# Preparing rows two chunks ahead, and 22 halves of shared-expert units beside the first group's maxima

## The reference

```python
xn = _layernorm(x)
q, k, v = (split_heads(xn @ W + b) for W, b in ((Wq, bq), (Wk, bk), (Wv, bv)))
scores = jnp.einsum('bhqd,bhkd->bhqk', q, k) / jnp.sqrt(dk)      # causal, then softmax
attn_out = merge_heads(softmax(scores) @ v) @ Wo + bo
...
logits = xn @ gate_w.T                                           # 4096 rows, 16 experts
topk_w, topk_idx = top_k(softmax(logits), 4); topk_w /= topk_w.sum(-1)
y = sum over the 4 experts e of topk_w * (silu(xn @ w_gate[e]) * (xn @ w_up[e])) @ w_down[e]
y = y + (silu(xn @ sw_gate) * (xn @ sw_up)) @ sw_down
return x + attn_out + y
```

## Time and profile before

| what | value |
|---|---|
| median of 3 runs | 1351.32 us (1346.31 to 1351.62) |
| the profiled execution | 1356.54 us, of which the span from the first to the last instruction 1354.9 us |
| busy share of the span | PE 74%, DVE 64%, ACT 48%, POOL 43% |
| chain that ended last, by engine | PE 53%, DVE 10%, another core or an unknown queue 10%, issue 9% |
| moved by DMA | 126.41 MB, mean 93 GB/s |
| mean granted clock of PE | 0.88 of full speed |

### The profile page before, as it was taken

How to read it: one execution, slowest core, us unless ns; L and a number is a source line. 1 busy time by engine, 2 the same in 40 slices (tenths; PEclk the granted TensorE clock), 3 DMA queues, 4 the chain that set the end, 5 groups by cost and what they waited for, 6 DMA issues and landing times.

```text
span 1354.9 us, 26394 instructions
## 1 busy us (share of the span) xinstructions
PE 1007.9 (74%) x8634; PEld 525.7 (39%) x8634; DVE 866.0 (64%) x1784; ACT 654.5 (48%) x1219; POOL 579.2 (43%) x531
## 2 busy tenths in 40 slices
PE   2788121010399999898998989998988989899885
PEld 1555010000144444444544444454444445444433
DVE  6888831000288887777777676676767676677553
ACT  3778100000154545565566666556666665566341
POOL 6333177776200000454366666435656553464100
PEclk9888555555599999899999999999989999899888
DMA  6899450010113131443545355354535353444702
GB/s 175 270 297 283 125 180 1 1 34 1 43 56 105 54 104 48 88 85 75 89 80 112 63 111 95 66 89 78 111 57 112 56 112 64 88 71 73 134 17 31
DMA packets 99484, 126.41 MB, mean 93 GB/s; under 512 B 24873, under 2 KB 83514, under 8 KB 98834
## 3 DMA queue, kind: packets, MB, share of 16 engines
q0 software_dynamic: 41632, 60.79, 25.0%
q1 hardware_dynamic: 57730, 63.99, 16.1%
HBM read 71.63 MB, written 57.80 MB: 96 GB/s over the span
## 4 chain that ended last, share of the span: by engine, by line
PE 53%; DVE 10%; another core or an unknown queue 10%; issue 9%; ACT 2%; SPq 1%; DMA 1%; POOL 0%; ACTq 0%; DVEq 0%
PE gup L1221 12%; PE pvp L1144 10%; PE outs L1248 9%; DVE part L1314 6%; PE smp L1100 6%; PE turn L1233 4%; PE stp L1125 4%; PE outs L1151 3%; PE turn L1191 3%; PE smp L1083 1%; ACT probs L1484 1%; DVE hf L1371 1%; DVE sg L1366 1%; DMA Qs<-nm 1%
## 5 line engine op out<-in xcount | busy, mean ns | idle before, releaser
L1484 ACT ACTIVATE probs<-stp 128x1024 f32<-128x1024 f32 (+1 forms) x320 | 300.4, 939 | 424.4 <-remote 205.2
L1314 DVE TENSOR_REDUCE part<-smp 128x2 f32<-128x256 f32 (+2 forms) x372 | 345.9, 951 | 140.0 <-remote 72.5
L942 POOL DMA_INDIRECT XG<-xrow_d,slots x144 | 146.8, 1019 | 247.0 <-DMA out<-Y 201.7
L1221 PE MATMUL gup<-gu_w,XC 128*128 (+1 forms) x1152 | 212.8, 321 | 32.7 <-issue 21.8
L1100 PE MATMUL smp<-Ks,Qs 48*128 48x128 f16 (+2 forms) x744 | 112.5, 341 | 103.7 <-DVE part L1314 52.4
L1248 PE MATMUL outs<-dn_w,h 88*128 (+1 forms) x1248 | 183.6, 280 | 0.1
L949 POOL DMA_INDIRECT out<-Y,slots x72 | 117.1, 1626 | 139.1 <-ACT Y L1517 107.8
L1144 PE MATMUL pvp<-probs,Vs 128*32 128x512 f32 (+3 forms) x1536 | 168.8, 512 | 0.8 <-DVE probs L1413 0.7
L949 POOL DMA_INDIRECT acc_d<-Y,slots x72 | 114.7, 1594 | 123.7 <-ACT Y L1517 104.6
L1221 PEld LDWEIGHTS gup<-gu_w,XC 128*128 128x128 f16 x1152 | 107.2, 99 | 96.1 <-issue 43.5
L931 POOL DMA_INDIRECT slot_d<-entry,slot_i x128 | 124.3, 971 | 41.6 <-issue 41.6
(11 more groups left out here) (170 smaller groups left out, 1109.6 us busy)
## 6 DMA issues: line engine op xcount, KB each, us to landing
rb<-rsum_d SPq DMA_DIRECT2D x60, 128.0 KB
Ks<-k_d SPq DMA_DIRECT2D x96, 64.0 KB
Qs<-q_d SPq DMA_DIRECT2D x96, 64.0 KB
v_d<-V SPq DMA_DIRECT2D x8, 544.0 KB, 4.6
Vs<-v_d SPq DMA_DIRECT2D x16, 272.0 KB, 3.0
acc_d<-YA SPq DMA_DIRECT2D x1, 4224.0 KB
X<-L_attn_x POOLq DMA_DIRECT2D x8, 512.0 KB, 5.0
xrow_d<-XR SPq DMA_DIRECT2D x8, 512.0 KB, 5.0
```

The costliest lines, as they stand in the source:

```text
L942: pool.indirect_dma_start(XG[:, q].rearrange("p a c t -> p (a c t)"), None, s.xrow_d, bass.IndirectOffsetOnAxis(ap=slots[:, r, 0:1], axis= ...
L1221: last = pe.matmul(gup[:, 0:2 * I], columns[:, a, h], weights_of(s.gu_w, e, b, h, slice(0, 2 * I)), start=n == 0, stop=n == 5)
L1314: last = dve.tensor_reduce(part[:, g % 2, k0 // CH, :, j, t], banks[:, :, col:col + w], AX.X, ALU.max)
L1484: act.activation(to, of, ACT.Exp, scale=float(DK) ** -0.5 / QS ** 2).then_inc(exp_done, 1)
```

## The change

In the preparation:

- The loop is written out (eight steps in Python), so `wait_apart` and its counters are gone.
- Rows are normalised two chunks ahead (`normalise` and `rows_low` for c+2), variances three ahead.
- The four Newton operations are POOL's, in its list ahead of the loads that belong to the step.
- The memset of Ks on POOL (128x6144) is six of 128x1024, at chunks 0, 1, 6 and 7. A spare square root loads ACT's table at the start.
- The shared expert's weights are converted in step 0, two experts each in steps 1 to 5 and three each in the last two (`SPLITS`); both conversions of an expert stand at the end of a step.

In attention and experts:

- The first PRE = 22 halves (12 first halves, units 0 to 11, and 10 second halves, units 0 to 9) are taken out of the slots and put one each behind the 18 pieces of group 0 and four steps more. The turn of the maxima comes in step 19.
- The planner divides the other 394 halves over the 320 slots. The last shared first half waits for slot 50 at the earliest (`READY`).
- SP loads XC and xs first, then serves the halves, sends the maxima, and only then issues the clear of acc_d and the copy to out.

```diff
-            per_slot = (sum(cost) + sum(fixed_work(g, n) for g, n in every)) / (len(every) - SPARE)
             first, second, i, used = {}, {}, 0, 0
+            for m in range(PRE):
+                (first, second)[halves[i][0]][-1, m] = halves[i][1]
+                i += 1
+            per_slot = (sum(cost[i:]) + sum(fixed_work(g, n) for g, n in every)) / (len(every) - SPARE)
             for k, x in enumerate(every):
                 used += fixed_work(*x)
                 for _ in range(2):
+                    if k < READY and i < len(halves) and halves[i] == (0, SU - 1):
+                        continue
...
-        LAG, SPARE = 2, 4
+
+        LAG, SPARE, PRE, READY = 2, 4, MP + 4, 50
...
+            for t in range(2):
+                shared_columns(t)
+                shared_rows(t)
+            for m in range(MP):
+                after_halves(-1, m)
+            send_max(0)
             sp.wait_ge(a_const, 2)
             sp.dma_start(s.acc_d.rearrange("(t p) d -> p t d", p=P),
                          YA[:, 0:1].broadcast_to([P, TT + 1, D])).then_inc(cleared, 16)
             sp.dma_start(s.out[ST * P:T, :], s.xf[ST * P:T, :]).then_inc(cleared, 16)
-            for t in range(2):
-                shared_columns(t)
-                shared_rows(t)
-            send_max(0)
+            for m in range(MP, PRE):
+                after_halves(-1, m)
...
-            for m in range(MP):
-                max_piece(0, m, (smp, stp)[m % 2], m - 1)
-            turn_max(0)
-            pe.wait_ge(red_done, MP)
             projected = 0
             youts = 0
+            for m in range(PRE):
+                if m < MP:
+                    max_piece(0, m, (smp, stp)[m % 2], m - 1)
+                if m == MP + 1:
+                    turn_max(0)
+                if (-1, m) in FIRST:
+                    gate_up(FIRST[-1, m])
+                else:
+                    z = SECOND[-1, m]
+                    turn_h(z)
+                    if z:
+                        down(z - 1, projected)
+                    youts = outs_before(z)
+            pe.wait_ge(red_done, MP)
```

More of the change, by code:

```diff
@@ L206, in flat, with one, expert_parts, later @@
             return w.rearrange("p c n -> p (c n)")
[L208 to L221, removed]
+        def one(t):
+            return t.rearrange("p o c n -> p (o c) n")
+        def expert_parts(e):
+            e = slice(e, e + 1) if isinstance(e, int) else bass.ds(e, 1)
+            return ([one(s.gu_w[:, e, a]).rearrange("p c (a i) -> p c a i", a=2) for a in range(2)],
+                    [one(s.dn_w[:, e, a]) for a in range(2)])
+        SPLITS = [[E, E + 1]] + [[2 * c - 2, 2 * c - 1] for c in range(1, NCH - 2)] + [[10, 11, 12], [13, 14, 15]]
+        ORDER = [e for step in SPLITS for e in step]
+        assert sorted(ORDER) == list(range(E + SH))
+        def later(c, ahead):
+            return c + ahead if c + ahead < NCH else None
         @block.sync
@@ L297, in _ @@
             last.then_inc(const_made, 1)
[L298 to L300 removed]
+            for k in range(SH):
+                load_expert(k)
+            newton(0)
             pool.memset(V[:, :, DK:DK + 1], 1.0).then_inc(v_ones, 1)
@@ L496, in step @@
                 low_half(c, 0)
                 low_half(c, 1)
-                if more(p, last):
-                    normalise(c + 1, 1 - p)
-                    rows_low(c + 1, 1 - p)
-                weights_low(c, 0)
+                if c and later(c, 2) is not None:
+                    normalise(c + 2)
+                if c == 0:
+                    rows_low(1)
+                    variances(2)
+                    dve.wait_ge(w_hi, 4)
+                    dve.scalar_tensor_tensor(out=g16[:, 1], in0=gT32[:, :, :], scalar=WS, in1=g16[:, 0],
+                                             op0=ALU.mult, op1=ALU.subtract).then_inc(w_lo, 1)
@@ L512, in _ @@
+                if later(c, 3) is not None:
+                    variances(c + 3)
+                first = sum(len(x) for x in SPLITS[:c])
+                for k in range(first, first + len(SPLITS[c])):
+                    weights_low(k)
+            variances(0)
+            normalise(0)
+            variances(1)
+            rows_low(0)
             for i in range(2):
@@ L557, in step @@
                     x.then_inc(qk_done, 1)
-                if more(p, last):
-                    turn(c + 1, 1 - p)
-                if began:
+                if later(c, 1) is not None:
+                    turn(c + 1)
+                if c:
                     pe.wait_ge(lg_out, c)
+                else:
+                    pe.wait_ge(w_lo, 4)
                 for j in range(TPC):
@@ L584, in _ @@
             last.then_inc(gt_done, 1)
-            turn(0, 0)
-            pe.wait_ge(w_lo, 4)
-            over_steps(pe, step)
+            pe.wait_ge(w_lo, 3)
+            for c in range(NCH):
+                step(c)
 def route(nc, s):
```

317 lines of the change are left out of this document (171 added, 146 removed).

## The result

The changed kernel takes 1395.07 us (median of 6, 1388.08 to 1405.23) against 1351.47 for the kernel before in the same series: a ratio of 1.0326, 95% interval 1.0279 to 1.0374. It is **slower by 3.3%**. The prediction had 1200 us. The profiled span is 1386.3 us, before 1354.9: 31.4 us more. The medians differ by 43.6 us: the profiled execution of after, 1388.08, was the shortest of its six and lies 7 us under their median, that of before (1356.54) lies 5 us above.

A forecast was written before the change was run, and what follows sets the result against it. PE bounds the loop (91% busy), with about 150 us of stall before it. Preparation 8 us shorter, maxima from 162 to 210, then 974 to 1184, plus 8 for the clear and 8 for waits: 1200 us, range 1175 to 1365.

The forecast's parts named there:

- The step that failed: Group 0's maxima: halves behind each piece keep PE busy, so the stall of about 150 us does not form; chance 0.43.
- two readings of the stall: Waits between 180 and 362 us, about 150 us: POOL's transfers alone cause them, or transfers together with an idle PE.
- my fourth case: Group 0's maxima: added halves bring more late handovers from PE, 10 us each; 1365 us, slower by 1.0%; chance 0.17.
- The preparation: Stage before routing: four parts summing to 8 us gained, routing starting at 134.5 instead of 142.50.
- Part (1): Start of the preparation: cutting the Ks memset into six and moving it gains 5.5 us to the first product.
- Part (3): Preparation chunks: rows made two chunks ahead remove PE's wait for rows of 25.9 us; 4 us gained.
- Part (4): End of the preparation: three experts in each of the last two steps with two stages cost 1.5 us, 0 to 7.
- "about 6" for that case: Preparation's gain in us if DVE and GpSimd share a locked port and moving the Newton operations is worth nothing.
- part (2): Preparation chunks: four Newton operations move from DVE to POOL, 0.7 us a chunk, hidden in POOL's 53.9 us wait.
- The steps of the maxima: Group 0's maxima with the 22 halves: 4 steps at 2.85 and 18 at 2.05 us, 48 us, slot 0 at 210.
- The loop: The 320 slots: 22 halves moved out save 25 us, between 20 and 29, at a PE 91% busy.
- Clear and copy: Clear of acc_d and copy of out, next to the loads of group 2's keys, add 8 us, 0 to 20.

The follow-up runs named there:

- e4: After, with POOL's 128 indirect transfers of the routing table made to wait for group 0's finished maxima: 1383.47 us, ratio 1.0269.
- e16: Before, with a memset of 0.54 us behind each of POOL's 128 indirect transfers, nothing of the change: 1226.5 us, ratio 0.9127.
- e10: After, with a memset of 1.40 us behind every second of POOL's 128 indirect transfers: 1283.13 us (one run), ratio 0.950.
- e7: After, with three SBUF stages for the experts' weights instead of two, nothing else: 1384.43 us, ratio 1.0238.
- e14: After, with 0.17 us memsets behind each indirect transfer, three weight stages and the clear ahead of the halves: 1346.75 us, ratio 0.999.
- e17: After, with 0.54 us memsets behind each indirect transfer, three weight stages, the early clear and READY = 62: 1222.45 us, ratio 0.9072.
- e2: The preparation of before with the attention and experts stage of after: 1390.3 us, ratio 1.0300.
- e8: After, with the clear of acc_d and copy to out issued behind the first loads of XC and xs, ahead of the halves: 1376.61 us, ratio 1.0197.
- e12: Before, with a memset of 0.17 us behind each of POOL's 128 indirect transfers, nothing of the change: 1335.17 us, ratio 0.988.
- run 77: Not a label but a count: PE ran 77 matmuls in 190:200 of after with 128 direct transfers replacing the indirect ones; 1252.67 us (one run), ratio 0.928.

## Why the prediction was wrong, point by point

**The step that failed** is "If the stall needs an idle PE, it does not form, because each of the 22 steps now puts 6 to 8 large matmuls behind each piece". I had two readings of the stall and preferred the one in which the loop's small waits spoke for a busy PE. e4 had a busy PE beside the same row and starved; e16 had the idle one beside a row with gaps and did not. So what PE does is not what tells the loop from the stretch 180 to 362. How POOL's transfers follow each other does differ: in the loop POOL is busy 45% of the time, in bursts (before has ten transfers from 552.14 to 566.29, 1.57 us apart on average and mixed with longer ones), where the row has 128 at 1.3; e10's pairs did no harm. That this difference is what saves the loop is argued from the table, no run changed the loop.

**The sign** was that of my fourth case, "the halves multiply the stall" (0.17, 1365 us), but its mechanism was only half right: handovers of PE are late indeed (86.6 us at 326.33), but it had put the whole delay there and let PE's own instructions flow. PE gets 0.4 to 0.5 matmuls a us, and the halves' matmuls use up the same ration as the pieces'. At 372.6 twelve of the 22 steps were done (PE's timeline), which is ten left where I had put 14 (and my own words there, eight steps done behind the first eight, would have left six). The remaining ten cost 17.7 us, not 34. The case missed by 16 us of span: it had the stall's end at 354, which was 372.6 (+18.6, the preparation's +10.8 in place of -8); 37.7 instead of 48 us from there to the free loop, the wait for XC included; and a loop and tail 16.9 shorter, not 25 (+8).

**The preparation**: -8 forecast, +10.8 measured. Part (1) came, 7.0 us for my 5.5: ACT's first product starts at 21.36 instead of 28.35, and L467 takes 0.17 us. Part (3) gave 0.3 instead of 4: the router's logits of the seventh chunk leave PSUM at 120.78 instead of 128.05, 7.3 us ahead. Part (4), the tail, was the mis-sized term: from there to the start of routing 18.1 us were lost, where I had put 1.5 (at most 7). I had counted one wait; there are two waits of ACT for a stage, 7.47 and 7.13 us, one in each of the last two steps, against 2.35 before:

```profile
132.80 0.79 ACT L394 ACTIVATE gu_w<-gu_stage 128x704 f16<-128x704 f32 x1 [7.47 <-DMA dn_stage<-L_ffn_w_down]
...
150.69 0.79 ACT L394 ACTIVATE gu_w<-gu_stage 128x704 f16<-128x704 f32 x1 [7.13 <-DMA dn_stage<-L_ffn_w_down]
```

and smaller ones of the kind before them. The waits of 15 to 165 us in after:

```profile
POOL nw L300 <- ACT rstd L372: 43.6, 6, 8.7
...
PE qk L579 <- ACT F L405: 29.5, 8, 9.3
ACT gu_w L394 <- DMA dn_stage<-L_ffn_w_down: 28.2, 10, 7.5
```

ACT waited 28.2 us at the weights (2.4 before), and what stands behind it in ACT's list, F, held PE (29.5). I had asked what PE waited for and let DVE's and the DMA's load bound the chunk; that ACT would wait for a stage in the middle steps too never entered the sum, and fits what part (3) lacked. The bound "POOL waited 53.9 us there for DVE anyway" was no cover either: POOL now waits 43.6 us for roots ahead of the loads. Three stages gave 7 to 11 us of it back (e7, e14, e17). The Trainium skill (SBUF — State Buffer, "SBUF: two separate sides") has DVE and GpSimd share one port pair under an exclusive lock, and I had concluded that moving the Newton step is then worth nothing. That was neither shown nor refuted here: its 0.7 us a chunk cannot be seen behind those waits. Nor did my "about 6" for that case follow, since the sum 5.5 + 4 - 1.5 has no term for part (2).

**The steps of the maxima**, 48 us forecast: where nothing starved PE (e4) its clock rose to 1.00 and 22 steps took about 40 (180.95 to some 220), so this term was near, 8 us too high. By the Trainium skill's rule (TensorE: Matmul & The Clock Gate, "What's actually happening") a busy array goes to the higher level; e4's 1.00 in 200:220 agrees, and after's 0.50 in 200:350 is the same rule with a starved one.

**The loop**, 25 us forecast: 16.9 (10.3 between the turns of groups 1 and 15: 850.0 before, 839.7 after; 6.6 in the rest). That is one pair of traces: from group 1's turn to the end after takes 928.6 us and before 942.3, but e2, e7 and e8, with the loop of after, take 944.0, 937.3 and 935.3, and e12, with that of before, 937.2. So the gain is small and its size open. **Clear and copy**, 8 forecast, 0 to 20 as bounds: 13 to 17 (the row at 410.31; e8). I had named it as a way to be wrong and given it half of its cost.

## What to carry to other kernels

When a wait has no releaser in the profile, find the engine that does something all the time beside it, and test by moving or thinning that, before building on a cure; here a 0.5 us memset behind each of 128 indirect transfers was worth 9%, and 22 halves of units put into the hole, with the clear and the copy behind them, cost 3% (e2), of which the late clear is about 1.3 by e8. Filling an idle stretch with work pays only if the engine is idle for want of work; if it is starved, the new work shares the same ration and comes on top at the end. Where loads go through two stages, count loads per step against stages, and see what stands behind the engine that waits for the third.

## What the runs showed of the hardware that I had not expected

An unbroken row of small indirect transfers issued by POOL, each busy for 0.96 us with 0.31 between, starves PE after about its first 10 us: PE had 42 matmuls in 181:191 of after and in 200:350 72 in 150 us, in steps of 2 to 3 us for one matmul or in whole groups after 15 to 16 us. The DMA engines are not busy meanwhile (share 0.03 in 200:350), and the low clock is no reason, since a gate_up of six matmuls takes 1.94 us at it. Nor is late code the reason in after: its DMA view of 200:350 lists these two queues alone (packets, MB, share), and none that carries instructions, so what PE ran there one by one had been loaded before.

```profile
q0 software_dynamic: 3698, 0.27, 2.3%
q1 hardware_dynamic: 432, 0.39, 0.9%
```

The same number of direct transfers, at twice the rate, let PE run 77 matmuls in 10 us. Between ACT and DVE I found no such delay (0.03 us from th to sg at 326.68), while PE's own signal to ACT came 86.6 us behind the end of its matmuls. Through what PE's instructions or its completions are held up, and so why 1.46 us from transfer to transfer is half enough, no run here shows; I leave it open.
